# A four-layer graph network on one core: in the first layer, half lanes and node ranges, one-hots built by ScalarE, and both next supertiles scored before this group's weights

## The reference

```
q, k, v = typed_linear(x) per node type          # 4 heads of 64
key_e = (k @ rel_att[edge_type])[edge_src];  val_e = (v @ rel_msg[edge_type])[edge_src]
att = (q[edge_dst] * key_e).sum(-1) * rel_pri[edge_type] / sqrt(64)
seg = edge_dst * 6 + edge_type                   # softmax inside each (dst, type)
w = exp(att - segment_max(att, seg)) / segment_sum(exp(...), seg)
t = mean over the types present of segment_sum(w * val_e, seg)
out = layernorm(alpha * typed_linear(t) + (1 - alpha) * x)
```

## Time and profile before

| what | us |
|---|---|
| three timed runs | 11175.55, 11189.87, 11194.74; median 11189.87 |
| profiled execution | 11198.95 |
| its span | 11197.0 |
| busy: PE, DVE, POOL, ACT | 7561.6, 5515.1, 4169.8, 2424.1 |
| typed pass with its start, until the combine | 598 to 2736 |
| combine | 2736 to 2855 |

### The profile page before, as it was taken

The page is one execution under the profiler, slowest core; times in us unless marked ns, Lnnn a source line. Parts: engine busy times, 40 slices in busy tenths (PEclk is TensorE's granted clock), DMA queues, the critical chain, the costliest instruction groups (busy, mean ns, idle before and its releaser), DMA issues. The chain is left out here.

```text
span 11197.0 us, 118660 instructions
## 1 busy us (share of the span) xinstructions
PE 7561.6 (68%) x28680; PEld 5418.4 (48%) x28681; DVE 5515.1 (49%) x9468; ACT 2424.1 (22%) x5021; POOL 4169.8 (37%) x4356
## 2 busy tenths in 40 slices
PE   5946666664634445799999999945656564666665
PEld 2535555553323334455555555524545453555554
DVE  2157787776232222455555555554444445444445
ACT  1212222221300000223332232322222221222221
POOL 0034444442046664133333332314444441444443
PEclk9978777777767776799999999966666666666666
DMA  2244444444023332233232332313333332333332
GB/s 78 99 129 140 141 141 141 138 141 106 27 70 89 89 89 59 73 91 89 88 93 85 92 93 84 92 49 99 98 92 95 94 97 61 97 98 96 101 100 75
DMA packets 396567, 1066.62 MB, mean 95 GB/s; under 512 B 93073, under 2 KB 132878, under 8 KB 396160
## 3 DMA queue, kind: packets, MB, share of 16 engines
q0 software_dynamic: 248064, 758.97, 24.2%
q1 hardware_dynamic: 148210, 305.04, 8.2%
HBM read 994.41 MB, written 69.29 MB: 95 GB/s over the span
## 5 line engine op out<-in xcount | busy, mean ns | idle before, releaser
L710 POOL DMA_INDIRECT st_rows<-g_table,st_stage_idx x1632 | 1554.7, 953 | 1779.2 <-DVE st_msg L2170 1294.1
L2322 PE MATMUL st_psM<-st_msg,st_hot 128*128 128x273 f32 x3264 | 1042.6, 477 | 452.9 <-DVE st_msg L2170 246.9
L800 POOL DMA_INDIRECT st_rows<-kv_table,st_stage_idx x816 | 948.7, 1163 | 1069.2 <-DVEq L983 821.9
L1451 DVE TENSOR_TENSOR st_pre<-st_psP,st_rows 128x512 f32<-128x512 f32 x816 | 563.2, 690 | 1120.9 <-PE st_psP L1544 748.5
L2322 PEld LDWEIGHTS st_psM<-st_msg,st_hot 128*128 128x128 f32 x3264 | 749.3, 236 | 683.9 <-issue 332.2
L656 POOL DMA_INDIRECT st_rows<-p_table,st_stage_idx x816 | 825.3, 1011 | 303.5 <-issue 220.9
L1544 PE MATMUL st_psP<-st_wb,st_eaT 64*128 64x512 f32 x1632 | 929.6, 650 | 0.9 <-ACT st_eaT L1489 0.8
L1557 PE MATMUL st_psC<-st_w,st_rT 128*128 128x256 f32 x3264 | 883.9, 395 | 33.7 <-ACT st_rT L1505 23.0
L710 POOL DMA_INDIRECT st_rows<-h_table,st_stage_idx x816 | 777.3, 953 | 263.3 <-issue 261.2
L2307 PE MATMUL st_psE<-dst_alpha,st_hotrow 128*128 x3264 | 638.1, 335 | 129.6 <-issue 97.0
L1359 PE MATMUL st_psM<-st_rows,st_hot 128*128 128x256 f32 x1632 | 449.2, 437 | 404.3 <-issue 179.7
(11 more groups left out here) (401 smaller groups left out, 12773.8 us busy)
## 6 DMA issues: line engine op xcount, KB each, us to landing
st_dst_row<-in_dst_row SPq DMA_DIRECT2D x308, 512.0 KB
kv_table<-st_rows_out SPq DMA_DIRECT2D x25, 1560.0 KB, 5.7
st_ea<-in_ea SPq DMA_DIRECT2D x103, 256.0 KB
st_rows<-g_table,st_stage_idx POOLq DMA_INDIRECT x1632
st_pens<-pen_table SPq DMA_DIRECT2D x102, 144.0 KB
st_rows<-kv_table,st_stage_idx POOLq DMA_INDIRECT x816
st_rows<-h_table,st_stage_idx POOLq DMA_INDIRECT x816
st_rows<-p_table,st_stage_idx POOLq DMA_INDIRECT x816, 3.7
```

The source lines that it names most:

```text
L710: pool.indirect_dma_start(out=rows[:, slot, j, :], out_offset=None, in_=table, in_offset=bass.IndirectOffsetOnAxis(ap=stage_idx[:, g, u * ...
L800: pool.indirect_dma_start(out=rows[:, slot, j, :], out_offset=None, in_=kv_table, in_offset=bass.IndirectOffsetOnAxis(ap=stage_idx[:, g, u ...
L1451: v.tensor_tensor(pre[:, j % DEEP, :], psP[j % 2][:, :], rows[:, u * SLOTS + j, :], ALU.add).then_inc(S["pre"], 1)
L2322: last = nc.tensor.matmul(out[:, 0:MSG_W], onehots[:, j, :], msg[:, n, j, :], start=(j == 0), stop=(j == SLOTS - 1))
```

## The change

- **Half lanes.** The scans run on 96 lanes of 512 edges (half, supertile, head, type) in place of 48 lanes of 1024. Each supertile then has four sides in place of two, so open rows are 24 of 128 columns (NQ = 104), and `typed_combine` works four sides.
- **Node ranges.** The window of 104 nodes starts at a supertile's own lowest node. Its queries are loaded per supertile (`query_rows`), and its sums are stored per supertile to acc_table (`store`), the second store behind the first one's landing. In `prepare` the table is zeroed by a DMA of 128 partitions.
- **One-hots by ScalarE.** `make_hot` on ACT makes 8 Squares of 128x128 and a Relu of 128x1024 for a supertile. ACT also copies the sums out of PSUM (`take_sums`); DVE's `combine` is gone.
- **Order.** DVE scores both supertiles of the next group before this group's weights, and spreads the types between the two messages. PE expands both before `turn_back`. There are 6 row buffers, and a loop turn has three groups.

The diff, cut to its core:

```diff
-NQ = 116
+NQ = 104
...
-    T_TURNS = T_GROUPS // 2
-    assert T_GROUPS == 2 * T_TURNS + 1
-    T_LANES = UT * H0 * RELS
+    T_TURNS = T_GROUPS // 3
+    T_LANES = 2 * UT * H0 * RELS
...
-    q_table = dram("q_table", [max(NPAD, NBQ * NQ), D])
-    acc_table = dram("acc_table", [NBA * NQ, SUM_W])
...
+                    sp.dma_start(acc_table[0:NPAD, :].rearrange("(b p) d -> p b d", p=P), NODE[:, :, 0:SUM_W]).then_inc(S["stored"], 16)
...
+                    v.tensor_scalar(minus_lo[:, 0:NS], psC[:, P:P + NS], -1.0, minus_p[:, :], ALU.mult, ALU.add)
+                    link(v.tensor_tensor(by_tile(typed_rel[:, :]), by_tile(db[:, :]), over_slots(psC[:, P:P + NS]), ALU.subtract))
...
+            def window(table, low, k):
+                at = low + k * NQ
+                at = nc.s_assert_within(at, 0, n_nodes, skip_runtime_bounds_check_because=BOUNDED)
+                return table[ds(at, NQ), :]
...
-                            pool.wait_ge(S["combined"], START + UT * q + u - 3)
+                            pool.wait_ge(S["summed"], START + UT * q + u - 4)
...
+                    def query_rows(s, u):
+                        _, _, low, _ = work_typed(sp, s + 1)
+                        sp.dma_start(q_rows[0:NQ, u, :], window(q_table, low, 0)).then_inc(S[f"q{u}"], 16)
...
+                    def store(q, u):
+                        s = UT * q + u
+                        x0, x1, low, more = work_typed(sp, s + 1)
+                        sp.wait_ge(S["opened"], START + s + 1)
+                        hold(sp, held)
+                        sp.wait_ge(S[f"acc{1 - u}"], 16 * q + 16 + 16 * u)
+                        sp.wait_ge(S["x_acc"], 16 + 16 * x0)
+                        hold(sp, held)
+                        sp.dma_start(window(acc_table, low, 0), outs[0:NQ, u, :]).then_inc(S[f"acc{u}"], 16)
+                        sp.dma_start(open_table[ds(s, 1), :, :].squeeze(0), outs[NQ:P, u, :]).then_inc(S[f"open{u}"], 16)
+                        with sp.If(more):
+                            sp.wait_ge(S[f"acc{u}"], 16 * q + 32)
+                            hold(sp, held)
+                            with sp.Fori(x0, x1) as x:
...
+                        for half in range(2):
+                            at = (half * UT + u) * H0
+                            values = rows[:, slot, half * HALF:(half + 1) * HALF, D:2 * D].rearrange("p j (h d) -> p j h d", h=H0)
+                            last = v.tensor_tensor(values, values, back_view()[:, :, at:at + H0].unsqueeze(3).to_broadcast(
+                                [P, HALF, H0, D // H0]), ALU.mult)
+                        last.then_inc(S["messages"], 1)
...
-                        link.turn()
-                        make_hot(q, 0)
                         segment_maxima(q)
-                        make_hot(q, 1)
+                        edge_scores(q + 1, 0, ahead_slot, ahead_turn)
                         segment_totals(q)
-                        if ahead:
-                            edge_scores(q + 1, 0, UT * (1 - g), i + g)
+                        link(edge_scores(q + 1, 1, ahead_slot + 1, ahead_turn))
                         edge_weights(q)
+                        messages(slot, 0)
+                        spread_types(q + 1)
+                        messages(slot + 1, 1)
                         for u in range(UT):
-                            messages(UT * g + u, u)
-                        if ahead:
-                            link(edge_scores(q + 1, 1, UT * (1 - g) + 1, i + g))
-                            spread_types(q + 1)
-                        for u in range(UT):
-                            combine(q, u)
...
+                            extra_hots(q, u)
...
-                        for g in range(2):
-                            group(2 * i + g, i, g, True)
-                    group(2 * T_TURNS, T_TURNS, 0, False)
...
+                        for g in range(T_SLOTS // UT):
+                            group(T_SLOTS // UT * i + g, g, i)
...
+                    def make_hot(q, u):
+                        s = UT * q + u
+                        act.wait_ge(S["summed"], START + s - 1)
                         hold(act, held)
-                        nc.scalar.copy(opens[96:P, u, :], sum_at[u][96:P, :]).then_inc(S["opened"], 1)
+                        link.turn()
+                        for j in range(SLOTS):
+                            last = nc.scalar.activation(hot[:, u, j, :], iota_row[:, :], ACT.Square, bias=minus_rel[:, ds(s * SLOTS + j, 1)])
+                        link(last)
+                        flat = hot[:, u, :, :].rearrange("p j n -> p (j n)")
+                        nc.scalar.activation(flat, flat, ACT.Relu, bias=ones_col[:, :], scale=-1.0).then_inc(S["onehot"], 1)
...
+                    def take_sums(q, u):
+                        s = UT * q + u
+                        x0, x1, _, more = work_typed(act, s + 1)
+                        act.wait_ge(S[f"acc{u}"], 16 * q + 16)
+                        act.wait_ge(S[f"open{u}"], 16 * q + 16)
+                        act.wait_ge(S["summed"], START + s + 1)
+                        hold(act, held)
+                        nc.scalar.copy(outs[:, u, :], psM[u][:, 0:SUM_W]).then_inc(S["opened"], 1)
...
+            SIDES = 4
...
-                    sp.dma_start(acc_table.rearrange("(b p) d -> p b d", p=NQ), ACC[0:NQ, :, 0:SUM_W]).then_inc(S["stored"], 16)
+                    sp.dma_start(NODE[:, :, 0:SUM_W], acc_table[0:NPAD, :].rearrange("(b p) d -> p b d", p=P)).then_inc(S["node_in"], 16)
                     with nc.allow_non_contiguous_dma(reason="first and last edge of a supertile"):
-                        for u in range(UT):
-                            for n, tile in enumerate((end_max, end_sum)):
-                                sp.dma_start(tile[:, :, :].rearrange("g (q u) k -> g u q k", u=UT)[:, u, :, :],
-                                             ends_table[n, u * G:(u + 1) * G, :, :]).then_inc(S["loads"], 16)
...
+                        for half in range(2):
+                            for u in range(UT):
+                                at = (half * UT + u) * G
+                                for n, tile in enumerate((end_max, end_sum)):
+                                    sp.dma_start(tile[:, :, half, :].rearrange("g (q u) k -> g u q k", u=UT)[:, u, :, :],
+                                                 ends_table[n, at:at + G, :, :]).then_inc(S["loads"], 16)
...
+                    for side in range(SIDES):
...
                     def turn_back(q):
                         pe.wait_ge(S["totalled"], START + q + 1)
                         pe.wait_ge(S["messages"], START + UT * q)
                         hold(pe, held)
-                        for j in range(SLOTS):
-                            last = nc.tensor.matmul(psW[:, j * SPACE:j * SPACE + BACK], both[0:TOT + T_LANES, j * P:(j + 1) * P],
-                                                    pick[0:TOT + T_LANES, :], start=(j == 0), stop=True, skip_group_check=True)
+                        for j in range(HALF):
+                            nc.tensor.matmul(psW[:, j * BACK:j * BACK + WT], ex[:, j * P:(j + 1) * P], pick[:, :],
+                                             start=(j == 0), stop=True, skip_group_check=True)
+                            last = nc.tensor.matmul(psW[:, j * BACK + WT:(j + 1) * BACK], tot[:, j * P:(j + 1) * P],
+                                                    ident[0:T_LANES, 0:T_LANES], start=False, stop=True, skip_group_check=True)
                         last.then_inc(S["back_ps"], 1)
 
-                    def group(q, g, ahead):
+                    def group(q, g):
                         turn_scores(q)
-                        if ahead:
-                            expand(q + 1, 0)
+                        for u in range(UT):
+                            expand(q + 1, u)
                         turn_back(q)
-                        if ahead:
-                            expand(q + 1, 1)
                         for u in range(UT):
                             scatter(q, u, UT * g + u)
 
-                    pe.wait_ge(S["q_in"], 16)
                     for u in range(UT):
                         expand(0, u)
```

More of the change, by code:

```diff
@@ L718, in gather_groups @@
                                               idx[:, ds((q + 1) * U * SLOTS, U * SLOTS)]).then_inc(S["idx_staged"], 1)
-    typed_landed = [top.enter_context(nc.semaphore(f"typed{n}")) for n in range(2 * UT)]
+    T_SLOTS = 6
+    typed_landed = [top.enter_context(nc.semaphore(f"typed{n}")) for n in range(T_SLOTS)]
     def typed_rows_in(eng, slot, i):
@@ L898, in spread_types, with extra_hots @@
+                        wide = [P, HALF, H0, RELS]
+                        for half in range(2):
+                            for u in range(UT):
+                                last = v.tensor_tensor(
+                                    et[:, :, half, u, :].rearrange("p j (h r) -> p j h r", h=H0),
```

(34 more changed lines are left out.)

550 lines of the change are left out of this document (277 added, 273 removed).

## The result

The changed kernel takes 10857.05 us (median of 4 runs, 10853.56 to 10899.33) against 11184.35 (4 runs, 11175.55 to 11194.74) on the same chip: a ratio of 0.9716, 95% interval 0.969 to 0.9741. The forecast was 10758 with a range of 10660 to 10890. The profiled execution spans 10851.7 us, 345.3 less than before.

| stretch | before | after | difference | forecast |
|---|---|---|---|---|
| start to the first scan (prepare, tables, start of the pass) | 687.6 | 642.1 | -45.5 | -53 |
| 50 groups, first scan to last | 2012.65 | 1814.4 | -198.2 | -397 |
| last scan to the end of the combine and the normalising | 470.3 | 487.2 | +16.9 | +18 |
| the four passes behind, whose code is the same | 8026.5 | 7908.0 | -118.5 | 0 |

The account below looks back on a forecast made before the run. No engine was full, DVE nearest at 79%, in a closed DVE-PE chain per group. Loop -397, start -57, pass end +3, combine +15 and prepare +4 gave -432 us: 10758 us against the median, range 10660 to 10890.

Parts of the forecast that it names:

- sum scans done: Loop group: two sum scans of 2.4 us, then 1.0 until the next scoring, reaching 12.0 us.
- message 0 done: Loop group on DVE: weights 2.09 us plus 0.2, then message 0 at half of 4.49, reaching 21.55 us.
- Extras: Typed pass loop: all 26 extra scatters go, at 8.8 us each, saving 229 us.
- Scoring supertile 0: Loop group on DVE: 4.78 us, plus 0.4 until its table entry is read, ending at 8.5 us.
- Scoring supertile 1: Loop group on DVE: 4.8 us plus 0.2 of link wait, ending at 17.0 us.
- PE's second expansion: Loop group: waits for DVE's reading of psE at 5 and 7.6 us, ends by 11, hidden beside scoring.
- Scatter 0: Loop group on PE: 6.1 us (bounds 3.7 and 6.4) at a lowered clock after 7 us idle, ending at 27.85.
- Scatter 1: End of loop group on PE: scatter 3.7 us, four transposes 0.5, and 0.3 to the next scan at 32.3.
- Rival 2: Loop: a new wait (gathers, ACT in order, remaining extras) keeps a group at 35.7 us, kernel 10928; chance 17%.
- Start: Start of pass: block load goes, first scan at 631 us in place of 687.6, -57 us (between -62 and -45).
- Combine: Combine stage: faster first load against more loads, open rows, sides and matmul rows, +15 us (bounds -15 and +40).
- end of the pass: After the loop: one more store chain, +3 us.
- prepare: Prepare stage: some five more operations of 816 columns, table zeroing hidden, +4 us (bounds +2 and +15).

Follow-up runs that it names:

- i_after: The changed kernel with 32-bit window tables kept and a max with 0 on the window numbers waited against; 9375.36 us, ratio 0.9451.
- c_before: The kernel before with its window tables in 16-bit numbers in place of 32-bit ones; 11536.73 us in one run.
- c_after: The changed kernel with its window tables in 16-bit numbers in place of 32-bit ones; 11295.03 us, ratio 1.0049.
- e6_dveload: The changed kernel with 16-bit window tables, without VectorE's table read before each scoring and the wait it feeds; 11258.95 us in one run.
- i_noextra: The changed kernel with 32-bit tables and all code for extra windows left out of the first layer's pass; 9347.27 us, ratio 0.9424.
- i_hwload: i_noextra with its gathers replaced by plain loads of as many bytes from fixed rows, issued by SyncE, output wrong; 9361.5 us in one run.

## Why the prediction was right, and where it was not

Step by step against i_after's group and the changed kernel's own (us from the first scan):

| step | forecast | i_after, 9911 kind | after, 11200 kind |
|---|---|---|---|
| scoring 0 done | 8.5 | 8.3 | 11.3 |
| sum scans done | 12.0 with the gap | 10.7, next scoring at 11.7 | 13.7 |
| scoring 1 done | 17.0 | 16.6 | 21.5 |
| message 0 done | 21.55 | 21.2 | 26.1 |
| scatter 0 done | 27.85 | 26.9 | 32.8 |
| next scan | 32.3 | 30.9 | 36.8 |

- **Extras**: right. All 26 went. By the first scans of the kernel before, its 24 groups without an extra take 35.9 us on average and its 26 groups with one 44.3, so an extra cost 8.4 us (forecast 8.8, from a single group of 35.7). Against a group without one the new group of 36.3 is 0.4 us longer, not 3.4 shorter.
- **The step that failed** is the scoring: "Scoring supertile 0: 4.78 ... 8.5" and "Scoring supertile 1: 4.8 ... 17.0", and with them "PE's second expansion ... beside it too". The count took TensorE's recorded ends for its real ones. Of the 4.5 us that the group above lacks, 2.8 came in scoring 0 and another 1.6 in scoring 1. The order before hid such lateness: 74 of the 199 updates of its expansion that can be paired were late, but VectorE had messages to make while TensorE expanded, and waited only 29.5 us (issue), 12.9 us (rows) and 8.5 us (TensorE) before L873.
- **Scatter 0** was sized at 6.1; it took 5.5 on the 9911 kind and 6.5 on the other, after 6.8 and 8.6 us of idling. Right as a mechanism: TensorE was at 1.2 GHz at its start, with 0.50 of the clock granted from 1342 to 1362 in the group shown (columns as in the earlier trace rows). **Scatter 1** with the transposes was 4.0, forecast 4.5.

```profile
1342.00:1362.00 20.00, 10.44 (x32) 8.33 (x31) 15.03 (x24) 4.31 (x4) 5.17 (x6) 0.50 0.47 142
```

- **Rival 2** named the outcome of the loop (a new wait eats the group's gain) but looked for it at the gathers, ACT and the extras; it was TensorE's expansion, held with 7 us of slack on paper.
- **Start**: the first scan came at 642.1 for 631, but the pass itself needed 49.3 us to it and not 33. Two waits put down to remote, 8.8 us before L951 and 8.9 before L992, cover that; the tables ahead of the pass, forecast as unchanged, took 9.5 us less and hid half of it. **Combine** +11.0 for +15, **end of the pass** +6.5 for +3, **prepare** +4.3 for +4.
- **What was forecast at nothing**: the unchanged passes. 75.7 of the 118.5 us lie in the first attention pass (from its first gather to the next pass's), 1917.0 us before and 1841.3 after, with 162 code packets before and 88 after. c_before and c_after show the same counts and 112.6 us. The code of that pass is the same and stands at other addresses; that this is the cause is argued, and no run tried it. Two numbers speak against the packets as such. In the second attention pass e6_dveload has 9 code packets and c_after 84, on the same chip, and the pass takes 1771.5 and 1773.2 us. And 38.3 more of the 118.5 us lie in the edge network (2884.3 us before, 2846.0 after), with 4 and 5 packets. So the cause of this part stays open.

The Trainium skill, "SBUF — State Buffer", section "SBUF: two separate sides", says that engine ports and DMA ports are disjoint, so that neither can slow the other. The 9911 kind agrees (none of 400 updates of matmuls in the loop of i_after came over 0.3 us after its recorded end). On the 11200 kind, in the loop after, 182 of the 196 updates of the expansion that can be paired with a recorded end (93%) came over 0.3 us after it, 2.9 us on average; a few updates are missing from the trace. The measurement decides that something holds TensorE there; which resource, it doesn't say.

The Trainium skill, "Runtime: NRT & Kernel Launch", section "Instruction fetch mechanics", warns that a branch out of the code at hand makes an engine wait for its next block. Such fetches did come, as 165 packets of 8 KB each, but in this loop they cost within 0.5 us a group, by i_after and i_noextra.

## What to carry to other kernels

Before an order is changed so that an engine waits for TensorE in the middle of a gather burst, look at when TensorE's updates reach their waiters and not at its recorded ends; where the waiter has other work, the lateness is invisible, and it appears when that work is moved. An edit that is held to be neutral needs a control of its own: a table's type cost 2.7 us a group beside the 4.0 that were being studied. And a total within the range proves no step; here 199 us that the loop did not give met 118.5 that nobody had counted on.

## What the runs showed of the hardware

- On the 11200 kind the late updates go with the gathers. In the profile before, behind the first layer, with the share of the DMA engines taken over the 3 us before each recorded end: 0 of 1687 updates were late with a share under 0.02, 0 of 211 beside plain loads alone (share 0.1 and more), and 423 of 668 where gathers took over 0.6, with 2.5 us on average over all 668. (The expectation of i_hwload speaks of 2000 beside plain loads; nearly all of those had no packets beside them.)
- In the loop after, with the share of gathers over the 5 us before: 0 of 135 late under 0.3, and 227 of 242 above. That is why the updates of scatters and transposes (L1170, L1195) were in time: gathers took 0.09 and 0.24 before them (medians), against 0.66 before those of the expansion. On the 9911 kind the same shares went with no late update.
- The same kernel before takes 9911 us on two chips, and 11184 and 11244 in the two measurements on the other kind. The change is worth 5.5% on the first kind (i_after) and 2.8% on the second.
- Reading four numbers of a table in SBUF, the on-chip memory, into an engine's registers took VectorE's sequencer 0.34 us from 32-bit numbers and 0.95 from 16-bit ones (TensorE 0.33 and 0.99).
